# Attention over 4096 tokens: half of the softmax denominators' partial sums added once more on VectorE before TensorE sums them

## The reference, cut to what matters

```python
x_flat = x.reshape(B, C, H * W).transpose(0, 2, 1)
Q, K, V = (split_heads(x_flat @ Wm + bm) for Wm, bm in ((Wq, bq), (Wk, bk), (Wv, bv)))
attn = jax.nn.softmax(jnp.einsum('bhnd,bhmd->bhnm', Q, K) * scale, axis=-1)
out = jnp.einsum('bhnm,bhmd->bhnd', attn, V)            # heads joined, then:
y = out @ Wo + bo + x_flat                              # and a layer norm with gamma, beta
```

## Time and profile before

| | |
|---|---|
| median of 3 runs | 6361.38 us (6359.47 to 6361.48) |
| the profiled execution: its time, its span | 6361.27 us, 6359.3 us |
| PE busy, share of the span | 5868.1 us, 92% |
| DVE | 5011.0 us, 79% |
| POOL | 4188.6 us, 66% |
| ACT | 3777.6 us, 59% |
| granted TensorE clock, mean | 0.955 |
| L399, ones products: number, busy | 4096, 533.1 us |
| L560, pair sums: number, mean of one | 2048, 1302 ns |
| L569, row maxima: number, mean of one | 4096, 682 ns |

### The profile page before, as it was taken

How to read it: one execution, slowest core, us unless ns; L and a number is a source line. 1 busy time by engine, 2 the same in 40 slices (tenths; PEclk the granted TensorE clock), 3 DMA queues, 4 the chain that set the end, 5 groups by cost and what they waited for, 6 DMA issues and landing times. The chain is left out here.

```text
span 6359.3 us, 93797 instructions
## 1 busy us (share of the span) xinstructions
PE 5868.1 (92%) x28212; PEld 2757.3 (43%) x28212; DVE 5011.0 (79%) x7254; ACT 3777.6 (59%) x7359; POOL 4188.6 (66%) x3147
## 2 busy tenths in 40 slices
PE   7999999999999999999999997888888888888887
PEld 3444444444444444444444442333333333333333
DVE  7777777777777777777777773798999998899988
ACT  3666566656666666666666665655556655556655
POOL 2677766776666776666677764566666666666666
PEclk9999999999999999999999998898989998889988
DMA  4011011011011011011000001000000000000000
GB/s 128 22 38 41 26 32 41 25 41 42 26 32 36 29 42 39 27 32 31 14 21 22 9 17 41 15 22 16 15 15 17 15 21 15 15 15 17 15 21 11
DMA packets 143428, 175.15 MB, mean 28 GB/s; under 512 B 64832, under 2 KB 88256, under 8 KB 141504
## 3 DMA queue, kind: packets, MB, share of 16 engines
q1 hardware_dynamic: 142944, 169.73, 9.4%
HBM read 109.11 MB, written 58.98 MB: 26 GB/s over the span
## 5 line engine op out<-in xcount | busy, mean ns | idle before, releaser
L560 POOL TENSOR_TENSOR sums<-exps 128x512 f32<-128x512 f32 x2048 | 2620.2, 1302 | 1309.9 <-ACT exps L493 1305.2
L569 DVE TENSOR_REDUCE mpart<-ps 128x1 f32<-128x512 f32 x4096 | 2539.8, 682 | 820.7 <-PE ps L369 820.7
L493 ACT ACTIVATE exps<-ps 128x512 f32<-128x512 f32 x4096 | 2127.8, 602 | 1404.5 <-PE ps L376 1404.1
L1218 POOL TENSOR_TENSOR hc<-hh,c_rep 128x512 f32<-128x512 f32 x1024 | 1490.0, 1458 | 825.8 <-DVE hh L1189 824.9
L369 PE MATMUL ps<-k_st,q_ring 96*128 96x512 f32 x4096 | 1753.7, 429 | 19.0 <-DMA k_st<-qk_split 9.4
L376 PE MATMUL ps<-q_ring,k_st 98*128 98x512 f32 x4096 | 1621.0, 397 | 4.0 <-ACT exps L493 3.6
L1189 DVE TENSOR_TENSOR_SCAN hh<-d_a,carry,ps 128x512 f32<-128x512 f32 x1024 | 1297.6, 1270 | 2.1
L369 PEld LDWEIGHTS ps<-k_st,q_ring 96*128 96x128 f32 x4096 | 774.7, 189 | 1065.6 <-DVE mpart L569 529.4
L1103 ACT ACTIVATE d_a<-ps,a_neg 128x512 f32<-128x512 f32 x1027 | 706.6, 688 | 726.3 <-PE ps L988 688.3
L387 PE MATMUL ps<-exps,v_ring 128*32 128x512 f32 x8192 | 1090.8, 605 | 0.0
L988 PE MATMUL ps<-s_dt,sel_g 128*128 128x512 f32 x1028 | 638.6, 621 | 324.0 <-ACT d_a L1103 319.7
(11 more groups left out here) (110 smaller groups left out, 3409.0 us busy)
## 6 DMA issues: line engine op xcount, KB each, us to landing
qk_split<-hilo SPq DMA_DIRECT2D x128, 256.0 KB, 2.3
q_ring<-qk_split SPq DMA_DIRECT2D x384, 64.0 KB, 2.0
k_st<-qk_split SPq DMA_DIRECT2D x45, 512.0 KB, 7.2
za<-z_ext SPq DMA_DIRECT2D x33, 320.0 KB, 3.1
zp<-z_ext SPq DMA_DIRECT2D x33, 320.0 KB, 4.0
xc<-in_x SPq DMA_DIRECT2D x32, 256.0 KB, 3.0
v_dram<-v_stage SPq DMA_DIRECT2D x32, 256.0 KB, 2.3
v_ring<-v_dram SPq DMA_DIRECT2D x16, 512.0 KB, 3.8
```

What stands on the lines that cost most here:

```text
L493: nc.scalar.activation(exps[:, u % 4, CH * half:CH * half + CH], a_bank(("exp", n, t)), ACT.Exp, scale=SCALE).then_inc(a_done, 1)
L560: pool.tensor_tensor(sums[:, u % 8, :], exps[:, u % 4, 0:CH], exps[:, u % 4, CH:2 * CH], ALU.add).then_inc(summed, 1)
L569: nc.vector.tensor_reduce(mpart[:, m % 2, t % 4, t // 4:t // 4 + 1], d_bank(("max", m, t)), AX.X, ALU.max).then_inc(d_done, 1)
L1218: pool.tensor_tensor(hc[:, g % NHC, :], hh[:, g % NHH, :], c_rep[:, p, :], ALU.mult).then_inc(hc_ready, 1)
```

## The change

In quads 1 to 4 VectorE adds the two pair sums of the quad before (`join_pairs`), so that `quads` holds four sums of four tiles each, over the slot's first 16 tiles. `sum_exps` is called in the quads behind `u = 4`, 5 and 7 (quads 5, 6 and, in the next slot, 0) in place of `u = 1, 3, 5, 7` (quads 2, 4, 6 and 0): the first of the three batches reads `quads`, the other two read the pair sums of the last 16 tiles as before. GpSimd waits for `quad_ready` before it writes a buffer of `sums` that an add reads, and `sum_used` counts 12 products a slot, not 16. `hilo` has one buffer for the splits, not two, so `high` waits for the stores of the chunk before.

```diff
-        hilo = sb("hilo", [128, 2, 2, 2, CH], F32R)
+        hilo = sb("hilo", [128, 2, 2, CH], F32R)
+        quads = sb("quads", [128, 4, CH])
...
                 def sum_exps(n, v):
-                    if v == 1 and n:
-                        pe.wait_ge(den_read, n)
-                    pe.wait_ge(summed, n * PAIRS + 2 * v + 2)
+                    if v == 4:
+                        if n:
+                            pe.wait_ge(den_read, n)
+                        pe.wait_ge(quad_ready, n * 4 + 4)
+                    else:
+                        pe.wait_ge(summed, n * PAIRS + 2 * v + 2)
                     for j in range(4):
                         u = 2 * v - 2 + j
-                        nc.tensor.matmul(ps[D * j:D * j + D, DEN_BANK, :], ones_d[:, :], sums[:, u % 8, :],
-                                         start=(v == 1), stop=(v == QUADS - 1)).then_inc(sum_used, 1)
+                        part = quads[:, j, :] if v == 4 else sums[:, u % 8, :]
+                        nc.tensor.matmul(ps[D * j:D * j + D, DEN_BANK, :], ones_d[:, :], part,
+                                         start=(v == 4), stop=(v == QUADS - 1)).then_inc(sum_used, 1)
...
-                        if 0 <= m < NS and u % 2:
+                        if 0 <= m < NS and u in (4, 5, 7):
                             sum_exps(m, u)
...
-                        if n * PAIRS + u >= 8:
-                            pool.wait_ge(sum_used, n * PAIRS + u - 7)
+                        if u >= 8:
+                            pool.wait_ge(quad_ready, n * 4 + (u - 8) // 2 + 1)
+                        elif n:
+                            pool.wait_ge(sum_used, n * 12 - 7 + u)
...
-                    dve.wait_ge(sum_used, n * PAIRS + PAIRS)
+                    dve.wait_ge(sum_used, n * 12 + 12)
...
+                def join_pairs(n, i):
+                    dve.wait_ge(summed, n * PAIRS + 2 * i + 2)
+                    nc.vector.tensor_tensor(quads[:, i, :], sums[:, 2 * i, :], sums[:, 2 * i + 1, :], ALU.add).then_inc(quad_ready, 1)
...
-                    if p >= 2:
-                        dve.wait_ge(split_stored[p % 2], 64 * (p // 2))
-                    nc.vector.tensor_copy(hilo[:, p % 2, i, 0, :], full[:, i, :]).then_inc(made, 1)
+                    if p:
+                        dve.wait_ge(split_stored[(p - 1) % 2], 64 * ((p - 1) // 2 + 1))
+                    nc.vector.tensor_copy(hilo[:, i, 0, :], full[:, i, :]).then_inc(made, 1)
...
                         if v == 1 and 0 <= n + 1 < NS:
                             shift_rows(n + 1)
+                        if 1 <= v <= 4 and 0 <= n < NS:
+                            join_pairs(n, v - 1)
```

More of the change, by code:

```diff
@@ L221, in layer0 @@
         names[:] = []
-        (d_ready, d_done, a_ready, a_done, av_done, out_read, summed, sum_used, den_read, mneg_ready, mrow_hi) = [
+        (d_ready, d_done, a_ready, a_done, av_done, out_read, summed, sum_used, den_read, mneg_ready, mrow_hi, quad_ready) = [
             sem(s) for s in ("d_ready", "d_done", "a_ready", "a_done", "av_done", "out_read", "summed", "sum_used", "den_read",
-                             "mneg_ready", "mrow_hi")]
+                             "mneg_ready", "mrow_hi", "quad_ready")]
         (made, split_ready, v_stored, recip_ready, squared, rstd_ready, scale_ready, z_ready, z_stored, f_in) = [
@@ L269, in store_projection @@
                         for part in range(2):
-                            sp.dma_start(qk_split[b, i, part, :, chunk(c)], hilo[:, p % 2, i, part, :].bitcast(F32)
+                            sp.dma_start(qk_split[b, i, part, :, chunk(c)], hilo[:, i, part, :].bitcast(F32)
                                          ).then_inc(split_stored[p % 2], 16)
@@ L592, in high @@
                     dve.wait_ge(a_done, a_at["proj", p, i] + 1)
-                    if p >= 2:
-                        dve.wait_ge(split_stored[p % 2], 64 * (p // 2))
-                    nc.vector.tensor_copy(hilo[:, p % 2, i, 0, :], full[:, i, :]).then_inc(made, 1)
+                    if p:
+                        dve.wait_ge(split_stored[(p - 1) % 2], 64 * ((p - 1) // 2 + 1))
+                    nc.vector.tensor_copy(hilo[:, i, 0, :], full[:, i, :]).then_inc(made, 1)
                 def low(p, i):
                     dve.wait_ge(made, 2 * p + i + 1)
-                    nc.vector.tensor_tensor(hilo[:, p % 2, i, 1, :], full[:, i, :], hilo[:, p % 2, i, 0, :].bitcast(F32), ALU.subtract
+                    nc.vector.tensor_tensor(hilo[:, i, 1, :], full[:, i, :], hilo[:, i, 0, :].bitcast(F32), ALU.subtract
                                             ).then_inc(split_ready, 1)
```

## The result

The changed kernel takes 6671.65 us (median of 4 runs, 6669.97 to 6674.44), the kernel before 6360.43 beside it: a ratio of 1.049, with a 95% interval of 1.0472 to 1.0508. The forecast was 6633 us, in a range of 6550 to 6722.

A forecast was written before the change was run, and what follows sets the result against it. PE was taken to bound the kernel; plain slots +175 us, finish +46, projection +53 and the last two slots -2 make +272 on 6361.27: 6633 us, range 6550 to 6722.

The forecast's parts named there:

- The hold: On DVE, an add that starts behind a GpSimd sum ends about 0.54 us after it, taking up to 1.7 us.
- The chain of quads: In plain slots each add keeps DVE 1.5 us behind PE through quads 2 to 5: +2.40 us a slot.
- D2: Start of DVE's first maximum in quad 2, forecast at P1 + 4.91 us, before at P1 + 3.98.
- P1: Start of PE's first row-maximum product in quad 1, from which the forecast counts a plain slot's times.
- D + 2.18: Start of GpSimd's second sum, counted from DVE's first maximum of the quad; forecast at 2.15 us after it.
- The finish slots: Slots with a finish: waits in quads 3 and 5 outweigh the saved batch, +1.6 us each, 46 us in 29 slots.
- rival 3: PE's waits lower its clock; up to 3.07 us more in each of 29 finish slots, 6722 us; chance 0.06.
- the forecast's own: The forecast's narrower range for the whole kernel, 6595 to 6675 us, from 0.05 us in eight terms of a slot.
- The projection slots: Slots with a projection: halves behind the adds lengthen quads 3 to 5, +2.2 us each, 53 us in 24 slots.
- What was costed at nothing: The single buffer of hilo, GpSimd's new waits for adds and PE's wait for quads were forecast to add no time.
- Rivals 1 and 2: Adds never wait, 6324 us or 6252, chance 0.08; or only the first ones are held, 6361 to 6565, chance 0.14.
- Rival 4: The hold lasts to the sum's very end, each add ending 0.69 us after it: 6698 us; chance 0.03.

The follow-up runs named there:

- e1: The changed kernel with each add replaced, from the second slot on, by a same-sized minimum of one SBUF and one PSUM operand: 6344.50 us.
- e4: The changed kernel with the four batches back in their old places over pair sums, the adds kept but their results unread: 6556.50 us.
- p0: The changed kernel with each add issued behind the first row maximum of its quad instead of the fourth: 6428.55 us.
- s7: The changed kernel with VectorE's scale moved from quad 2 to quad 6 and ScalarE's affine from quad 3 to 7: 6580.71 us.
- e3: The kernel before with only the single buffer of hilo: 6367.71 us.
- e2: The changed kernel without its adds, quads being set once and the waits for the adds removed: 6247.77 us.
- w0: The changed kernel, adds behind first maxima of quads 2 to 5, batches in 6, 7, 0, scale in 6, projection halves in 7 and 0: 6253.57 us.
- t6: The changed kernel, adds behind first maxima of quads 2 to 5, batches in 6, 7, 0, scale in 6, projection halves in 6 and 7: 6301.31 us.
- q0: The changed kernel with adds behind first maxima of quads 2 to 5, batches in quads 6, 7, 0, scale in 6, affine in 7: 6330.11 us.

## Why the prediction was right, and what was mis-sized

**The hold.** Right. The one row of `scaled` at 2069.19 carried it: 0.54 us past the sum's end there, 0.55 in the changed kernel. e1 shows that the second SBUF operand is the cause and not the add's length or place. By the Trainium skill (SBUF — State Buffer, Who interferes with whom) a VectorE instruction with at most one SBUF input, outside its two-port modes, doesn't contend with GpSimd; e1's 0.666 us in the median, beside a sum, agrees.

**The chain of quads.** Right to some hundredths. D2 was to be P1 + 4.91 and is 4.93; a quad was to take 3.89 and takes 3.93, since GpSimd's second sum starts at D + 2.18 and not 2.15, and the add ends 0.55 after it; quad 1 to quad 6 were to take 19.82 and take 19.97. A plain slot loses 2.54 us, not 2.40 (the first slot of all gains 1.53). Of the 39 us that were missing, the 73 plain slots make 6, the projection slots 5 and the finish slots 26.

**The finish slots.** The term that was mis-sized: +1.6 was forecast, 24 of them that follow a finish lost 2.50 in the mean, the four others with maxima 2.26. The waits were right: the lag of quad 3 came as worked out (`scaled` takes 1.78 us behind the add; quad 3 lasts 4.71, forecast 4.70), and slots without a fall of the clock lost about 1.5. What the sum had at nothing, and kept as rival 3 alone, is the clock. PE in such a slot, with its longest waits, and the windows before and at the fall (the third figure from the end of a row is the granted clock):

```profile
...
2015.17 0.50 PE L370 MATMUL ps<-k_st,q_ring 96*128 96x512 f32 x1 [1.37 <-DVE mpart L576]
...
2019.11 0.50 PE L370 MATMUL ps<-k_st,q_ring 96*128 96x512 f32 x1 [0.59 <-DVE mpart L576]
...
2020.83 1.85 PE L388 MATMUL ps<-exps,v_ring 128*32 128x512 f32 x8
2022.61 0.80 PE L370 MATMUL ps<-k_st,q_ring 96*128 96x512 f32 x1
```

```profile
...
2254.81:2285.68 30.87, 28.55 (x158) 13.22 (x154) 26.48 (x40) 17.62 (x33) 20.25 (x17) 1.00 0.06 17
2019.00:2020.90 1.90, 1.79 (x8) 0.66 (x12) 1.90 (x5) 0.78 (x2) 1.38 (x2) 1.00 0.00 0
2020.98:2024.39 3.41, 3.41 (x12) 1.50 (x7) 2.19 (x3) 1.71 (x3) 0.85 (x1) 0.50 0.00 0
...
```

PE waits 1.37 us in quad 3 and 0.59 in quad 4; then the granted clock is 0.50, the lower level of 1.2 GHz, for 3.41 us, and a product that took 0.50 takes 0.80. From its first slot on the first layer has 33 such stretches, 24 in slots that follow a finish, two in other finish slots, seven in projection slots and none in the 72 plain ones, where PE waits about 0.6 us in each of four quads. Of the slots after a finish, the one without a fall took 34.74 us, 1.46 more than before, against 35.78 in the mean: about 1.1 us in each of the others, 25 us. With the two finish slots (35.3 us with a fall, 33.79 without) and the seven (33.69 for 33.47) the clock cost some 30 us, by this comparison of slots; no run took the clock's fall away and left the waits. e4 has the same comparison: its 9 finish slots with a fall took 36.53 us in the mean, the 15 without 34.91, behind the same waits. Rival 3 was given 0.06 as the place of the forecast; it was an addition to it, at a third of the price feared (1.1 us a slot, not 3.07). The tail of the layer, busy for 59.68 of 65 us at 1.00, did not speak for the slots: its waits are of 0.2 to 0.3 us. What decides whether a slot has a fall stays open. The longest wait alone doesn't: in the two other finish slots with a fall none is over 0.61 us, and in e4 none of the 24 slots after a finish waits over 0.62. One of its nine falls, with the longest wait before it:

```profile
...
2002.80 0.50 PE L370 MATMUL ps<-k_st,q_ring 96*128 96x512 f32 x1 [0.62 <-DVE mpart L573]
...
```

```profile
...
2004.78:2008.19 3.41, 3.41 (x17) 0.73 (x10) 1.29 (x1) 1.07 (x2) 0.74 (x1) 0.50 0.00 0
...
```

p0's finish slots wait 0.56 and 0.93 and have none; and seven of 22 projection slots had one in the changed kernel, none in s7, where they are the same.

The measured time lies in the range, and 3 us inside the forecast's own. That the own range held is partly luck: it stands for errors of 0.05 us in the terms of a slot, and most of what was missing is the clock. (Its working is off as well: 0.05 us in eight terms of 126 slots make 50 us, not 40.)

**The projection slots.** +2.2 was forecast, 22 of them lost 2.37, those without a fall 2.30; quads 3 to 5 take 3.53, 4.53 and 5.13 there, for 3.5, 4.5 and 5.1. **What was costed at nothing** cost nothing: e3 shows it for `hilo`, e2 for the moved batches. GpSimd's new waits are read from the row of L567 in the changed kernel: of the 1601.2 us of idle time before its sums 1596.1 ended with an exponential. PE's products over `quads` have no idle time before them. **Rivals 1 and 2** would have needed an add ahead of the second sum in quads 1 to 4; that is e4's quads 3 and 4, where the batches left VectorE the time. **Rival 4** (held to the very end) falls: 0.55 us after the sum's end, not 0.69.

The adds' mean was to be over 1.1 us and is 1.40; PE's waits were to be 0.8 us in quads 2 to 5, of which 0.54 to 0.60 stand as idle time before the fourth maximum; the rest is the overlap with the product before it that is lost (0.17) and the later start of the product behind it (0.11).

## What to carry to other kernels

Before work is given to an engine that looks idle on average, place it among the instructions of the engine that shares its reads, and see who starts first: here an add that came 0.21 us behind a sum took 1.62 us and one that came 0.10 us ahead of it (e4) 0.69, and four adds and three batches a slot made the kernel 4.9% slower or, with the adds ahead of the sums and the other work moved as in w0, 1.7% faster. A ring of three banks is a deadline for whoever reads it; list every product that waits on that ring, not the next one alone, when work is put in front of a read. A lag that repeats itself (the late maximum makes the sum late, and the sum then holds the add) doesn't decay as long as each quad brings another add, so one late start can cost a whole chain.

## What the runs showed of the hardware that was not expected

A copy with rounding, with one SBUF input, is held as well: in the changed kernel the high halves (L606) take 980 ns in the mean, against 514 before and 417 in w0, where they lie ahead of the sums. Of the 48, 23 take 0.41 us; the other 25 start some 0.5 us behind a sum and take 1.50. One of these, with its sum:

```profile
...
L606 DVE CAST hilo<-full 128x512 fp32r<-128x512 f32 x48 | 47.1, 980 | 0.0
...
```

```profile
...
130.74 1.50 DVE L606 CAST hilo<-full 128x512 fp32r<-128x512 f32 x1
...
```

```profile
...
130.22 1.73 POOL L567 TENSOR_TENSOR sums<-exps 128x512 f32<-128x512 f32 x1
```

It ends at 132.24, 0.29 us after the sum (131.95). The same copy ahead of the sums is the 0.42 us of w0.

PE's granted clock can fall in a stretch in which it works for most of the time and never waits longer than 1.4 us: from the first slot on the first layer has 33 falls of 3.41 us in the changed kernel, 16 in e4, 2 in s7, 1 in t6, and none in the kernel before, w0, e1, e2, e3, p0 or q0.
